# Second attention: where the high part of the exponentials is made (VectorE cast, or a second ScalarE exponential)

## The reference

```
# 1  group norm, q/k/v projections, full attention over 1024 tokens, output projection, residual
x = x + proj(softmax(q^T k / 16) v)
t = tokens(x)                                    # 1024 x 256
# 2  second attention, on layer-normed tokens
n = layer_norm(t)
c = n / |n|                                      # unit rows
s = (c c^T)^2                                    # 1024 x 1024, symmetric
t = t + softmax(s) n
# 3  feed-forward with a sign matrix, clip, rounding to sevenths, residual
t = t + quantise(layer_norm(t) sign(w) mean|w| + b)
```

## Time and profile before

| | us |
|---|---|
| runs of the kernel (3): median, lowest, highest | 1810.67, 1809.89, 1815.19 |
| the profiled execution: its time | 1809.76 |
| the profiled execution: its span, first to last instruction | 1808.0 |
| PE busy in the span | 1748.7 |
| DVE, ACT, POOL busy in the span | 1315.6, 943.2, 718.9 |
| mean granted clock of PE | 0.997 |

### The profile page before, as it was taken

How to read it: one execution, slowest core, us unless ns; L and a number is a source line. 1 busy time by engine, 2 the same in 40 slices (tenths; PEclk the granted TensorE clock), 3 DMA queues, 4 the chain that set the end, 5 groups by cost and what they waited for, 6 DMA issues and landing times.

```text
span 1808.0 us, 34783 instructions
## 1 busy us (share of the span) xinstructions
PE 1748.7 (97%) x11938; PEld 1606.1 (89%) x11938; DVE 1315.6 (73%) x2580; ACT 943.2 (52%) x1476; POOL 718.9 (40%) x1334
## 2 busy tenths in 40 slices
PE   7999999999999999999999999999999999999997
PEld 6898988988889998898988989889898988988887
DVE  6767767677686777767777686776867867677675
ACT  3645646456463554635446354563645546456462
POOL 0442615327152361623616245261542615327161
PEclk9999999999999999999999999999999999999999
DMA  3404123050330504205041140512404033050230
GB/s 122 121 24 152 36 92 117 23 179 7 104 104 26 183 0 128 80 36 173 0 151 58 58 151 3 157 48 70 139 23 154 32 97 112 23 182 4 89 99 24
DMA packets 97055, 152.88 MB, mean 85 GB/s; under 512 B 11648, under 2 KB 70400, under 8 KB 97024
## 3 DMA queue, kind: packets, MB, share of 16 engines
q1 hardware_dynamic: 97024, 152.48, 26.7%
HBM read 76.95 MB, written 75.50 MB: 84 GB/s over the span
## 4 chain that ended last, share of the span: by engine, by line
PE 57%; issue 19%; POOL 11%; DVE 8%; ACT 4%; DMA 1%; POOLq 0%; SPq 0%; ACTq 0%; DVEq 0%
PE wide L371 22%; PE narrow L371 5%; PE narrow L473 4%; PE narrow L475 4%; PE narrow L474 4%; PE wide L473 4%; PE wide L475 4%; PE wide L474 3%; PE turn L543 2%; DVE gn_stats L973 2%; POOL ln_r L1277 2%; PE turn L582 2%; PE turn L426 2%; PE turn L573 2%; POOL sq_root L1291 1%
## 5 line engine op out<-in xcount | busy, mean ns | idle before, releaser
L371 PE MATMUL wide<-xn_hi,prob 128*128 128x512 f32 x1024 | 303.5, 397 | 0.3 <-ACT expo L747 0.3
L1274 POOL TENSOR_TENSOR ln_v<-ln_mv,ln_eps 128x2 f32<-128x2 f32 (+2 forms) x128 | 31.6, 247 | 542.6 <-DVE ln_mv L1042 332.6
L371 PEld LDWEIGHTS wide<-xn_hi,prob 128*128 128x128 f32 x1024 | 185.3, 188 | 39.2 <-ACT expo L747 0.7
L786 ACT ACTIVATE ln<-tok,ln_shift,ln_r 128x256 f32<-128x256 f32 x128 | 68.4, 593 | 264.1 <-POOL ln_shift L1279 264.1
L754 ACT ACTIVATE prob<-e_back 128x1024 fp32r<-128x1024 f32 x112 | 118.5, 1058 | 156.0 <-DMA e_back<-e_scratch 142.6
L747 ACT ACTIVATE expo<-wide,neg_max 128x1024 f32<-128x1024 f32 x128 | 142.2, 1111 | 96.0 <-DVE neg_max L1010 96.0
L1010 DVE TENSOR_REDUCE neg_max<-wide 128x1 f32<-128x1024 f32 x128 | 155.1, 1212 | 40.0 <-PE wide L371 40.0
L1319 POOL TENSOR_TENSOR carrier_p<-ones 128x1 f32<-128x1 f32 x60 | 11.6, 193 | 415.6 <-DVE y_sb L1090 413.1
L1017 DVE STREAM_TRANSPOSE x_norm<-expo 128x1024 f32<-128x1024 f32 x112 | 139.1, 1242 | 49.2 <-ACT expo L747 48.8
L371 PE MATMUL wide<-xn_lo,prob 128*128 128x512 f32 x512 | 160.7, 394 | 0.0
L1022 DVE TENSOR_TENSOR prob<-e_back,prob 128x1024 fp32r<-128x1024 f32 x112 | 135.8, 1213 | 31.2 <-ACT prob L754 30.9
(11 more groups left out here) (179 smaller groups left out, 5445.2 us busy)
## 6 DMA issues: line engine op xcount, KB each, us to landing
e_scratch<-x_norm SPq DMA_DIRECT2D x112, 512.0 KB, 3.0
e_back<-e_scratch SPq DMA_DIRECT2D x448, 128.0 KB, 3.2
x_raw<-in_x SPq DMA_DIRECT2D x32, 512.0 KB, 3.6
out<-y_sb SPq DMA_DIRECT2D x32, 512.0 KB, 3.6
tok<-in_L_conv_qkv_w SPq DMA_DIRECT2D x1, 768.0 KB, 6.6
ln<-in_L_conv_proj_w SPq DMA_DIRECT2D x1, 256.0 KB, 6.4
ln<-in_L_ffn_weight SPq DMA_DIRECT2D x1, 256.0 KB, 3.4
out_bias<-in_L_conv_proj_b SPq DMA_DIRECT2D x1, 128.0 KB, 3.8
```

Source lines behind the costliest of these rows:

```text
L371: mm = pe.matmul(o, lhsT, r, start=first and i == 0, stop=last and i == len(parts) - 1)
L786: act.activation(ln2[:, n], tok[:, n], ACT.Identity, bias=ln2_shift[:, n:n + 1], scale=ln2_r[:, n:n + 1]).then_inc(ln2_made, 1)
```

## The change

ACT takes the exponential of the squared scores twice. The first, new one writes straight into `prob[:, 0, J]` with fp32r output and gives `p_hi_made`; after a wait for it the second one works in place in `expo` as before and gives `e2_made`. DVE's nine casts per image are gone. DVE `e2_last_lo` and POOL `e2_lo` now wait for `e2_made`, which implies the high part. `turn_e2` on PE still waits for `e2_made`, so now for the second exponential.

```diff
@@ act: exp2(b, u)
                 act.activation(e, wide[J % 2][:, offset(J) + c0:offset(J) + c1], ACT.Square).then_inc(sq2_made, 1)
                 act.wait_ge(sq2_made, NP * b + u + 1)
+                act.activation(prob[:, 0, J, c0:c1], e, ACT.Exp).then_inc(p_hi_made, 1)
+                act.wait_ge(p_hi_made, NP * b + u + 1)
                 act.activation(e, e, ACT.Exp).then_inc(e2_made, 1)
@@ dve
-            def e2_hi(b, u):
-                J, c0, c1 = PARTS[u]
-                dve.wait_ge(e2_made, NP * b + u + 1)
-                dve.tensor_copy(prob[:, 0, J, c0:c1], expo[:, J % DEEP, c0:c1]).then_inc(p_hi_made, 1)
-
             def e2_last_lo(b, u):
                 J, c0, c1 = PARTS[u]
-                dve.wait_ge(p_hi_made, NP * b + u + 1)
+                dve.wait_ge(e2_made, NP * b + u + 1)
                 dve.tensor_sub(prob[:, 1, J, c0:c1], expo[:, J % DEEP, c0:c1],
                                prob[:, 0, J, c0:c1].bitcast(F32)).then_inc(p_last_made, 1)
@@ dve: front
                 residual1(b, 4)
-                e2_hi(b, 0)
-                e2_hi(b, 1)
                 residual1(b, 5)
...
-                e2_hi(b, 2)
                 cosT_lo(b, 2)
                 e2T_parts(b, 2)
...
-                e2_hi(b, 3)
                 cosT_lo(b, 3)
                 e2T_parts(b, 3)
...
-                e2_hi(b, 4)
                 e2T_parts(b, 4)
                 cosT_lo(b, 4)
-                e2_hi(b, 5)
                 e2T_parts(b, 5)
-                e2_hi(b, 6)
-                e2_hi(b, 7)
                 e2_last_lo(b, 7)
                 e2T_parts(b, 6)
-                e2_hi(b, 8)
                 e2_last_lo(b, 8)
@@ pool: e2_lo(b, J)
-                pool.wait_ge(p_hi_made, NP * b + J + 1)
+                pool.wait_ge(e2_made, NP * b + J + 1)
```

More of the change, by code:

```diff
@@ L1049, in cosT_lo, with e2_last_lo @@
                                tokT_hi[:, :, n0 * P:n1 * P].bitcast(F32)).then_inc(cosT_made, 1)
-            def e2_hi(b, u):
+            def e2_last_lo(b, u):
                 J, c0, c1 = PARTS[u]
                 dve.wait_ge(e2_made, NP * b + u + 1)
-                dve.tensor_copy(prob[:, 0, J, c0:c1], expo[:, J % DEEP, c0:c1]).then_inc(p_hi_made, 1)
-            def e2_last_lo(b, u):
-                J, c0, c1 = PARTS[u]
-                dve.wait_ge(p_hi_made, NP * b + u + 1)
                 dve.tensor_sub(prob[:, 1, J, c0:c1], expo[:, J % DEEP, c0:c1],
```

## The result

The changed kernel takes 1825.76 us (median of 4 runs, 1824.73 to 1827.18) against 1810.28 us for the kernel before (4 runs, 1809.11 to 1815.19): a ratio of 1.0081, 95% interval 1.0061 to 1.0101, so 15.5 us slower. The forecast was 1819.5 us with the sign right; the loss is 1.8 times the 8.8 us that the sum gave, and the time lies 0.8 us above the upper end of the range. The profiled execution took 1825.09 us, span 1823.3 us.

What follows compares the result with a forecast made beforehand. The prediction took PE to bound the kernel, busy 1748.7 of 1808.0 us. A delay of 0.55 us in each of 16 images gave 8.8 us more, so 1819.5 us against 1810.67, with a range of 1813 to 1825.

Steps and rivals of the forecast that it cites:

- the sum: Whole kernel: 16 images, each 0.55 us later at `turn_e2(5)`, give 8.8 us more.
- Bound, and `turn_e2(1)`: PE bounds the kernel; its first wait per image stays, at most 0.1 us longer.
- both covers: ACT's waits for POOL absorb added exponential time: about 0.77 us ahead of `turn_e2(1)`, 1.18 of 1.21 ahead of `layer_norm1(4)`.
- Price and place on ACT: Each new exponential costs its duration plus a 0.03 us gap: 0.55 to 0.99 us for rows 2 to 6.
- `scores2(4)`: Without DVE's cast, `cosT_lo(2)` starts earlier, so PE's `scores2(4)` gains 0.27 us of its 0.5 us wait.
- `turn_e2(4)` and `turn_e2(5)`: PE waits for ACT's second exponential: starts 0.06 to 0.22 us later, then 0.52 to 0.68, taken as 0.55.
- `turn_e2(6)` and row 7: After `turn_e2(5)` PE waits no more; POOL's `e2_lo(6)` ends near 879.2, wanted by `product2(0)` at 880.3.
- Rival 2: ACT later than forecast, `cos_x` at 867.79, cover at `turn_e2(1)` 0.1 short: 0.68 to 0.9 us per image; chance 0.18.
- Rivals 1: Row 7's lower part late, POOL's `e2_lo(6)` holding `e2_last_lo(7)`: up to 0.5 us per image, 1827 us; chance 0.04.
- 3: POOL and DVE meet differently, shortening PE's first wait: 6 us back, 1813.5 us; chance 0.2.
- 4: DVE's free time decides: `scores2(4)` gains 0.27 to 0.5 us per image, nothing given back, 1802.4 to 1806.3; chance 0.06.

Runs made afterwards that it cites:

- the run with the short exponential: Kernel before, casts kept, plus one extra 128-column exponential on ACT ahead of row 5's, its output overwritten by DVE's cast: 1812.48 us, ratio 1.0012.
- DVE's relief alone: Changed kernel without its first exponentials, so the lower triangle gets no high part from ACT or DVE: 1804.79 us, ratio 0.9970.
- row 4 alone: Kernel before, with only row 4's high part made by a second exponential on ACT instead of DVE's cast: 1818.09 us, ratio 1.0038.

## Why the prediction was right in sign and short in size

- **Bound, and `turn_e2(1)`**: right. PE's first wait is 20.8 us in all, against 22.6; both covers held. The 1.8 us can't be put down to the change: with the casts in place, the run with the short exponential has 20.6.
- **Price and place on ACT**: right. Row 4 was made 12.61 us behind `turn_e2(1)`, forecast 12.60 to 12.76; from the start of `cosT_hi(4)` to row 5 it takes 2.85 us where it took 1.96, 0.89 more for a forecast of 0.88.
- **`scores2(4)`**: right. 4.1 us of waiting instead of 8.3; DVE's relief alone gave 0.27 in the stage, forecast 0.27. At `turn_e2(2)` the row was forecast 0.2 us late; the load is 0.47 late there, by the same misreading as below, and `group_means` covers it.
- **`turn_e2(4)` and `turn_e2(5)`**: the right two places, mis-sized. The step that failed is "PE gets there at 870.53 - 0.27 = 870.26" and its twin, "PE wanted it at 873.65: a slack of 0.46". 870.53 and 873.65 are where the chain hands over from the matmuls before; the row is wanted at the weight load, 0.27 and 0.34 earlier. The slack of row 5 was 873.31 - 873.23 = 0.08 us, not 0.42. In the chain the first start (0.08 late for 0.06 to 0.22) and the wait at `turn_e2(5)` (0.47 for 0.46) came as forecast, but each of the two steps was itself 0.22 us longer, which the prediction had at nothing: 0.08 + 0.22 + 0.47 + 0.22 = 0.99 us per image, measured 1.00. So `turn_e2(5)` started 0.77 late, for 0.52 to 0.68. Added up over the 16 images, the stages are 16.4 us longer, what lies ahead of and between them is 2.5 shorter (1.8 of it at PE's first wait), and the end behind the last one 1.3 longer, which the kernel without any high part has too (1.2): the span grew by 15.3.
- **`turn_e2(6)` and row 7**: right, no wait. `e2_last_lo(7)` was held by POOL's `e2_lo(6)`:

```profile
885.48 0.90 DVE L1056 TENSOR_TENSOR prob<-expo,prob 128x512 fp32r<-128x512 f32 x1 [2.08 <-ACT expo L812]
```

```profile
883.71 2.12 POOL L1297 TENSOR_TENSOR prob<-expo,prob 128x896 fp32r<-128x896 f32 x1 [0.93 <-ACT expo L812]
```


It takes 0.90 us and ends 0.55 behind POOL's 885.83, where an undisturbed one takes 0.68; over the 32 of these subtractions the mean rose from 692 to 790 ns. `product2(0)` has started at 885.10 and wants block 7 at 887.6, so nothing waits. That a DVE instruction with two SBUF inputs and a POOL instruction that reads SBUF hold each other off is what the Trainium skill, SBUF — State Buffer, section Who interferes with whom, says. The trace agrees in kind; held off for the whole of POOL's instruction, it would have ended at 885.83 + 0.68 = 886.51, and it ended 0.13 us earlier.

- **Rival 2** foresaw 0.68 to 0.9 per image for another reason (covers too short). Its size was near, its cause was not there: `cos_x` came at the early end of the forecast. Rivals 1, 3 and 4 did not happen in the changed kernel. 1 has its like when the casts stay in, for 0.20 us per image; 4's gain exists, but only where the rows are not made late.

The Trainium skill, TensorE: Matmul & The Clock Gate, section Step-by-step: what each phase is for, says that PE can pull a weight load ahead of matmuls in flight. This trace agrees: 0.27 and 0.34 us ahead where the row is there, 0 where it isn't. The Trainium skill, Perfetto Trace Analysis, section Tensor Engine Instruction (MATMUL, LD_WEIGHTS), adds that the ends of matmuls in a profile are a model, which speaks against reading a slack off them.

The parts add up once it is seen that DVE's relief acts in two places. Alone it gives 0.27 us, at `scores2(4)`. In the changed kernel PE waits for ACT at `turn_e2(4)`, so that gain is lost there, and what counts is the earlier `len_i`: row 4 is made at 12.60 us instead of the 12.78 of row 4 alone. So the relief is worth 0.18, and 0.49 + 0.69 - 0.18 = 1.00, as measured; with 0.27 the sum would be 0.91. Row 6 is no part of it: `turn_e2(6)` loads its weights at 884.06, 0.39 us after row 6 is there.

Not settled: why the load leads its own first transpose by 0.11 us in one place and by 0.18 in another.

## What to carry to other kernels

The slack of data that a transpose or matmul uses as weights is counted to the weight load before it, not to the matmul; here 0.42 us of apparent slack was 0.08, and the list of PE's waits grew by 3.7 of the 15.3 us that were lost. When a second result is wanted from the same input, make first the one that the bounding engine waits for: with the casts gone in both, the same amount of work on ACT left the kernel 15 us slower in front of that result and 5.6 us faster behind it. Work taken off an engine that isn't the bound gains only where that engine, or one that it was slowing, was late: here 0.27 us per image for 5.8 us of casts.

## What the hardware showed that was not expected

A missed run-ahead of the weight load costs some 0.22 us per step, for four transposes as for five (0.44 to 0.66, 0.55 to 0.77), on top of the wait in the matmul rows; a load late by only 0.28 us showed no wait there and cost 0.16. And with two waits of PE close together (1.10 of 2.00 and 0.53 of 1.70 us busy) the granted clock fell to 0.50 in 12 of 16 images, some 20 us in all, although the waits of PE in total had hardly grown. The kernels before and after, whose longest wait in an image behind the first is 1.5 us, show no such fall until the end.
